# Rows of q and k moved straight from SBUF to the heads' rows, without a DRAM scratch, in a two-layer attention and pooling kernel

## The reference

```python
# layer 0, per batch: 16 heads of 16, s = side input, x = input
q = (s + b_self) @ Wq + bq            # 256 x 256, scaled by 1/4
k = (x + b_prev) @ Wk + bk;  v = x @ Wv + bv
k_self = (s + b_self) @ Wk + bk;  v_self = s @ Wv + bv
score_prev = q k^T (keys past the length masked);  score_self = sum(q * k_self) per head
w = softmax([score_prev, score_self]);  x1 = x + (w_prev @ v + w_self * v_self) @ Wo + bo
# layer 1: pooling with one of three masks per batch
t = tanh(x1 @ W1 + b1) . v;  p = softmax(masked t, per row);  out = x1 + (p @ x1) / count
```

## Time and profile before

| | us |
|---|---|
| median of three runs (range) | 279.0 (278.47 to 279.12) |
| the profiled execution: its own time | 281.62 |
| span from first to last instruction in its profile | 279.9 |
| TensorE busy / VectorE / ScalarE / GpSimd | 238.4 / 184.4 / 156.6 / 76.3 |
| mean granted TensorE clock | 0.950 of 2.4 GHz |
| busy in DMA queue q1, share of 16 engines' span | 44.6% |

### The profile page before, as it was taken

How to read it: one execution, slowest core, us unless ns; L and a number is a source line. 1 busy time by engine, 2 the same in 40 slices (tenths; PEclk the granted TensorE clock), 3 DMA queues, 4 the chain that set the end, 5 groups by cost and what they waited for, 6 DMA issues and landing times.

```text
span 279.9 us, 6089 instructions
## 1 busy us (share of the span) xinstructions
PE 238.4 (85%) x2100; PEld 187.4 (67%) x2100; DVE 184.4 (66%) x384; ACT 156.6 (56%) x297; POOL 76.3 (27%) x87
## 2 busy tenths in 40 slices
PE   2986898599979999999999989999999769886732
PEld 2984787367758777877788768777787455563622
DVE  2659655457469758875887588758985885335631
ACT  4351223376477557755785667557856546772430
POOL 8026011013025103610451035103511330316111
PEclk9999669599999999999999999999999997999977
DMA  5469636913865096609560946096409410011011
GB/s 152 103 235 233 138 112 182 210 31 115 242 142 188 5 248 134 228 16 252 119 227 20 256 108 225 18 246 118 150 33 261 95 72 2 8 34 37 0 40 37
DMA packets 28021, 35.50 MB, mean 127 GB/s; under 512 B 4440, under 2 KB 24416, under 8 KB 28000
## 3 DMA queue, kind: packets, MB, share of 16 engines
q1 hardware_dynamic: 27360, 33.12, 44.6%
q0 software_dynamic: 640, 2.10, 2.0%
HBM read 20.26 MB, written 14.69 MB: 125 GB/s over the span
## 4 chain that ended last, share of the span: by engine, by line
PE 59%; DVE 13%; DMA 9%; issue 8%; ACT 5%; SPq 3%; POOL 1%; ACTq 0%; DVEq 0%; POOLq 0%
PE ps_any L1080 20%; PE ps_any L1134 10%; PE ps_max L1108 9%; PE ps_any L1087 6%; DMA k_rows<-k_spill 5%; PE ps_exp L1121 4%; DVE s_max L887 4%; DMA k_spill<-k_lo 3%; PE ps_any L1184 3%; PE ps_any L1240 2%; DVE bv_cast L854 2%; SPq L418 1%; ACT pt L623 1%; PE ps_any L1200 1%; PE ps_any L1166 1%
## 5 line engine op out<-in xcount | busy, mean ns | idle before, releaser
L887 DVE TENSOR_REDUCE s_max<-ps_max 128x4 f32<-128x1024 f32 x64 | 78.1, 1220 | 25.1 <-PE ps_max L1108 25.1
L623 ACT ACTIVATE pt<-ps_exp 128x1024 f32<-128x1024 f32 x64 | 65.6, 1025 | 50.1 <-PE ps_exp L1121 49.5
L1108 PE MATMUL ps_max<-k_rows,q_rows 49*128 49x256 f32 x256 | 33.7, 343 | 13.0 <-DMA k_rows<-k_spill 7.2
L1108 PEld LDWEIGHTS ps_max<-k_rows,q_rows 49*128 49x128 f32 x256 | 20.2, 194 | 24.6 <-DVE s_max L887 10.4
L1134 PE MATMUL ps_any<-pt,v_aug 128*32 128x256 f32 x512 | 36.0, 401 | 0.0
L1121 PE MATMUL ps_exp<-q_rows,k_rows 51*128 51x256 f32 x256 | 27.0, 288 | 2.3 <-ACT pt L623 2.3
L578 POOL TENSOR_TENSOR attn<-num,rden 128x256 f32<-128x256 f32 x16 | 9.6, 621 | 54.0 <-DVE rden L1030 54.0
L1121 PEld LDWEIGHTS ps_exp<-q_rows,k_rows 51*128 51x128 f32 x256 | 20.3, 191 | 4.1 <-ACT pt L623 2.7
L569 POOL TENSOR_TENSOR prod_lo<-prod,prod_hi 128x512 fp32r<-128x512 f32 x8 | 10.3, 1282 | 42.2 <-ACT prod_hi L714 42.2
L1080 PE MATMUL ps_any<-st_hi,w_hi 128*128 128x256 f32 x64 | 20.9, 326 | 0.3 <-DVE st_lo L912 0.3
L1134 PEld LDWEIGHTS ps_any<-pt,v_aug 128*32 128x32 f32 x512 | 13.7, 112 | 10.5 <-issue 1.3
(11 more groups left out here) (145 smaller groups left out, 605.3 us busy)
## 6 DMA issues: line engine op xcount, KB each, us to landing
q_rows<-q_spill SPq DMA_DIRECT2D x32, 192.0 KB, 4.4
k_rows<-k_spill SPq DMA_DIRECT2D x32, 192.0 KB
q_spill<-q_hi SPq DMA_DIRECT2D x16, 256.0 KB, 2.5
k_spill<-k_hi SPq DMA_DIRECT2D x16, 256.0 KB, 2.5
s_sb<-in_fside_BxSxS SPq DMA_DIRECT2D x8, 256.0 KB, 3.7
x_sb<-in_x SPq DMA_DIRECT2D x8, 256.0 KB, 3.2
q_spill<-q_lo SPq DMA_DIRECT2D x8, 256.0 KB, 2.2
k_spill<-k_lo SPq DMA_DIRECT2D x8, 256.0 KB, 3.1
```

The source lines that it names most:

```text
L623: nc.scalar.activation(pt[:, 2 * j % 8:2 * j % 8 + 2], ps_exp[:], ACT.Exp).then_inc(p_ready, 1)
L887: nc.vector.tensor_reduce(s_max[:, j // MJ, :, :, j % MJ].rearrange("p t e -> p e t"), ps_max[:], AX.X, ALU.max).then_inc(max_found, 1)
L1108: last = pe.matmul(ps_max[:, e, t], q_rows[par][rows, j, P * t:P * t + P], k_rows[par][rows, j, :], start=True, stop=True)
```

## The change

The weight columns of q and k are ordered so that the half m of the projection is g, and a partition is (e, d, j within the half). A band of a head's rows then is 64 partitions of one part tile, and a DMA can move it from SBUF to SBUF: 64 partitions by 256 numbers become 16 partitions by 4 pairs by 256. The scratch, its spills and their semaphores are gone. Each batch now takes 12 such DMAs of 64 KB for q and 12 for k, next to the same two for the mask, where it took 6 spills and 8 placements before. q's g = 0 rows are sent ahead of the first half of the maxima, the others behind them in the order k 0, q 1, k 1. Tiles q_hi, q_lo, k_hi, k_lo are free again when both halves are placed, not when they are spilled. The biases of q and k come by four DMAs, not two. VectorE's set-up moves from the end of period -1 into steps 2, 4, 6 and 10 of period 0, and `bv_product` into its step 5.

```diff
-            def spill(i, k, parts, hi_done, lo_done, pattern, dram, placed, placed_per, spilled):
-                n_parts = held(count(i, k, 1, 1))
-                if (n := held(count(i, k, placed_per, 0))) is not None:
-                    for half in placed:
-                        sp.wait_ge(half, n)
...
-            def place(dram, rows, placed, g):
-                for e in range(2):
-                    sp.dma_start(rows[64 * e:64 * e + ROWS, MJ * g:MJ * g + MJ].bitcast(F32),
-                                 dram[e].rearrange("c (d j) t -> (c d) j t", d=DH)[:, MJ * g:MJ * g + MJ]
-                                 ).then_inc(placed[g], 16)
+            def place(part, rows, placed, g, threes):
+                for c in threes:
+                    for e in range(2):
+                        sp.dma_start(rows[64 * e + DH * c:64 * e + DH * c + DH, MJ * g:MJ * g + MJ].bitcast(F32),
+                                     part[P // 2 * e:P // 2 * e + P // 2, g, :].bitcast(F32)
+                                     ).then_inc(placed[g], 16)
+            def place_q(i, k, g):
+                par = k % 2
+                n_parts = held(count(i, k, 1, 1))
+                n_scored = held(count(i, k, NJ, MJ * (g + 1) - 2 * NJ))
+                if n_scored is not None:
+                    sp.wait_ge(scored, n_scored)
+                elif g == 0:
+                    sp.wait_ge(rows_one, par + 1)
+                sp.wait_ge(q_copied, n_parts)
+                place(q_hi, q_rows[par], q_placed, g, (0, 1))
+                sp.wait_ge(q_lo_done, n_parts)
+                place(q_lo, q_rows[par], q_placed, g, (2,))
+            def place_k(i, k, g):
...
+                sp.wait_ge(k_hi_done, n_parts)
+                place(k_hi, k_rows[par], k_placed, g, (0, 2))
+                if isinstance(i, int) and 2 * i + k == 0:
+                    sp.wait_ge(masks_stored, 16)
+                sp.dma_start(k_rows[par][R_MASK:R_MASK + 65:64, MJ * g:MJ * g + MJ].bitcast(F32), mask
+                             ).then_inc(k_placed[g], 16)
+                sp.wait_ge(k_lo_done, n_parts)
+                place(k_lo, k_rows[par], k_placed, g, (1,))
...
                 if live(*nxt):
-                    spill(*nxt, (q_hi, q_lo), q_copied, q_lo_done, (0, 0, 1), q_spill, q_placed, 32, q_spilled)
+                    place_q(*nxt, 0)
+                if live(*nxt) and not live(*b):
+                    place_q(*nxt, 1)
                 if live(*b):
                     place_max(*b, 0)
                 if live(*nxt):
-                    spill(*nxt, (k_hi, k_lo), k_hi_done, k_lo_done, (0, 1, 0), k_spill, k_placed, 48, k_spilled)
...
+                    place_k(*nxt, 0)
+                    if live(*b):
+                        place_q(*nxt, 1)
+                    place_k(*nxt, 1)
...
                 for n, vec in enumerate((bq, bk)):
-                    sp.dma_start(bqk_raw[:, n, :], vec.rearrange("(j e d) -> d j e", e=2, d=DH)
-                                 ).then_inc(bias_loaded, 16)
+                    for g in range(NM):
+                        half = vec.rearrange("(g n) -> g n", g=NM)[g]
+                        sp.dma_start(bqk_raw[:, n, g:g + 1], half.rearrange("(j f) -> f j", j=MJ).unsqueeze(2)
+                                     ).then_inc(bias_loaded, 16)
...
-                    if first and s == STEPS:
-                        cast_bv()
-                        weight_lo(3)
-                        setup_pooling()
-                        dve.wait_ge(bv_product_ready, 1)
-                        nc.vector.tensor_tensor(bias_out[:], bo_wide[:], ps_exp[:, 0, 0], ALU.add
-                                                ).then_inc(bias_out_done, 1)
+                    if isinstance(i, int) and 2 * i + k == 0:
+                        if s == 2:
+                            cast_bv()
+                        if s == 4:
+                            weight_lo(3)
+                        if s == 6:
+                            dve.wait_ge(bv_product_ready, 1)
+                            nc.vector.tensor_tensor(bias_out[:], bo_wide[:], ps_exp[:, 0, 0], ALU.add
+                                                    ).then_inc(bias_out_done, 1)
+                        if s == 10:
+                            setup_pooling()
...
+                    if isinstance(i, int) and (2 * i + k, s) == (0, 5):
+                        bv_product()
...
-                if first:
-                    bv_product()
```

More of the change, by code:

```diff
@@ new lines, in place_k @@
+            def place_k(i, k, g):
+                par = k % 2
+                mask = row(mask_dram, i, k).unsqueeze(0).unsqueeze(0).broadcast_to([2, MJ, S])
+                n_parts = held(count(i, k, 1, 1))
+                sp.wait_ge(k_hi_done, n_parts)
[6 more added lines that the diff above has]
+                place(k_lo, k_rows[par], k_placed, g, (1,))
@@ L530, in _, with split_lo @@
                                     pattern=[[-P, KB], [1, S]], channel_multiplier=-1).then_inc(pool_const, 1)
-            def split_lo(i, k, full_done, hi_done, full, hi, lo, lo_done, spilled):
+            def split_lo(i, k, full_done, hi_done, full, hi, lo, lo_done, placed):
                 pool.wait_ge(full_done, count(i, k, 1, 1))
                 pool.wait_ge(hi_done, count(i, k, 1, 1))
-                if (n := count(i, k, 48, 0)) is not None:
-                    pool.wait_ge(spilled, n)
+                if (n := count(i, k, 96, 0)) is not None:
+                    for half in placed:
+                        pool.wait_ge(half, n)
                 nc.gpsimd.tensor_tensor(lo[:], full[:], hi[:].bitcast(F32), ALU.subtract).then_inc(lo_done, 1)
@@ L555, in period @@
                     for c in at("q_lo", i, k, s):
[L556 removed]
+                        split_lo(*c, q_full_done, q_copied, q_full, q_hi, q_lo, q_lo_done, q_placed)
                     for c in at("x1_lo", i, k, s):
@@ L635, in weight_hi @@
                 for kb in range(KB):
-                    dst, src = w_hi[:, n, kb], w_raw[:, n, kb]
                     if n < 2:
[L638 to L641, removed]
+                        last = nc.scalar.activation(
+                            w_hi[:, n, kb].rearrange("p (g f j) -> p g f j", g=NM, j=MJ),
+                            w_raw[:, n, kb].rearrange("p (g j f) -> p g f j", g=NM, j=MJ),
+                            ACT.Copy, scale=QSCALE if n == 0 else 1.0)
+                    else:
+                        last = nc.scalar.activation(w_hi[:, n, kb], w_raw[:, n, kb], ACT.Copy)
+                    last.then_inc(w_hi_ready, 1)
             def period(i, k):
@@ L694, in period @@
                         act.wait_ge(k_ready, count(*c, 1, 1))
-                        if (n := count(*c, 48, 0)) is not None:
-                            act.wait_ge(k_spilled, n)
+                        if (n := count(*c, 112, 0)) is not None:
+                            for half in k_placed:
+                                act.wait_ge(half, n)
                         for m in range(2):
@@ L769, in q_copy @@
                 last.then_inc(q_full_done, 1)
-                if (n := count(i, k, 48, 0)) is not None:
-                    act.wait_ge(q_spilled, n)
+                if (n := count(i, k, 96, 0)) is not None:
+                    for half in q_placed:
+                        act.wait_ge(half, n)
                 for m in range(2):
@@ L793, in weight_lo @@
                     if n < 2:
-                        for e in range(2):
-                            hi, lo = (w[:, n, kb].rearrange("p (e d j) -> p e d j", e=2, d=DH)[:, e]
+                        for g in range(NM):
+                            hi, lo = (w[:, n, kb].rearrange("p (g f j) -> p g f j", g=NM, j=MJ)[:, g]
                                       for w in (w_hi, w_lo))
-                            src = w_raw[:, n, kb].rearrange("p (j e d) -> p e d j", e=2, d=DH)[:, e]
+                            src = w_raw[:, n, kb].rearrange("p (g j f) -> p g f j", g=NM, j=MJ)[:, g]
                             last = nc.vector.scalar_tensor_tensor(
@@ L990, in period @@
                         dve.wait_ge(k_hi_done, count(*c, 1, 1))
-                        if (n := count(*c, 48, 0)) is not None:
-                            dve.wait_ge(k_spilled, n)
+                        if (n := count(*c, 112, 0)) is not None:
+                            for half in k_placed:
+                                dve.wait_ge(half, n)
                         for m in range(2):
@@ L1160, in self_scores @@
             def self_scores(bank):
-                by_block = bank[:, 0, 0:2 * H].rearrange("p (g t e j) -> p t e g j", g=NM, t=KB, e=2)
+                by_block = bank[:, 0, 0:2 * H].rearrange("p (g t j) -> p t g j", g=NM, t=KB)
                 for t in range(KB):
-                    for e in range(2):
+                    for g in range(NM):
                         for part in (prod_hi, prod_lo):
```

(2 more changed lines are left out.)

18 lines of the change are left out of this document (5 added, 13 removed).

## The result

| | before | after |
|---|---|---|
| median of the runs taken side by side (range), four each | 278.7 us (276.6 to 279.1) | 297.0 us (293.9 to 298.0) |
| ratio, with its 95% interval | | 1.065 (1.056 to 1.075): slower |
| the profiled execution: its time / its span | 281.62 / 279.9 | 298.02 / 296.3 |
| mean granted TensorE clock in it | 0.950 | 0.918 |

Forecast was 273.0 us, with a chance of 0.11 for slower; the time lies 19 us above the range. Of the rivals only D, "283.6 or more", pointed this far, by a mechanism that is not the one found.

A forecast was written before the change was run, and what follows sets the result against it. It took TensorE, busy for 85% of the span, as the bound, with waits for k rows. Terms -1.1 + 1.7 + 0.9 - 3.15 - 1.8 - 2.1 - 0.4 = -5.95 us took 279.0 to 273.0 us; range 269.3 to 278.0.

The forecast's parts named there:

- D: Rival for the row DMAs: write rate falls in full proportion, 0.92 us a DMA; 283.6 us or more, chance 0.10.
- what stands last in SP's queue: SP's queue: free 12.5 us after the copy, the second maxima next, landing in time by half a microsecond.
- From the third period on ... what the change does to DMAs there is hidden: TensorE has no idle time worth the name there; periods 3 and later stay at 27.8 us.
- Issue of 0.50 us: SP's issuing of each new 64 KB row DMA: 0.50 us taken, with 0.65 kept as a rival.
- rival E: SP's queue: issuing costs 0.65 us a DMA, the second maxima come late; 279.5 us, no change, chance 0.10.
- Landing of 2.6 us: Each row DMA lands 2.6 us from the start of its issue, within 2.2 to 4.2.
- B: Rival for the row DMAs: narrow writes pace the queue at 0.61 us a DMA; 274.5 us, chance 0.15.
- Waits of periods 1 and 2: TensorE's waits for k rows at these periods' starts: both go, 3.15 and 2.12 us.
- The start: Period 0's start: last k_lo issued at 25.1, landed at 27.7 against 28.18; max0 gains only 0.5 us.
- The clock: TensorE in period 1: without the wait at 49.2 the clock should not fall at 51, worth 1.8 us.
- Set-up in period 0: Moved work costs 1.7 us for `bv_product` and 0.9 us for the small set-up ahead of max5's reduction.
- the gain of 1.1 us: Start of period 0: without set-up ahead, the first Q product starts at 30.1 and not 31.20.

The follow-up runs named there:

- e1: The changed kernel with the reload of x issued right behind the next batch's loads, ahead of the row DMAs: 286.2 us, ratio 1.023 to the kernel before.
- e4: The kernel before with nine more 8 KB DMAs, which nothing reads, ahead of the reload in each period: 293.6 us, ratio 1.046.
- e5: e4 with the reload of x moved ahead of the row DMAs, so the nine no longer precede it: 282.5 us, ratio 1.005.
- e6: e1 with k's g = 0 rows sent ahead of q's g = 1 rows in period -1 too: 281.0 us, ratio 1.004 to the kernel before.
- e3: The changed kernel with VectorE's set-up and bias product put back at the end of period -1: 298.1 us, ratio 1.068 to the kernel before.
- e8: The kernel before with groups of four DMAs of several forms behind its last store: SBUF-to-SBUF forms took 0.59 to 0.62 us to issue.
- e2: The kernel before with only VectorE's set-up and the bias product moved into period 0: 280.7 us, ratio 1.008.
- e11: The kernel before with further DMA groups behind its last store: the 256 KB spill stayed below 0.5 us to issue, 128 into 128 partitions in SBUF took 0.60.

## Why the prediction was wrong, step by step

**The failed step: what stands last in SP's queue.** The prediction worked out when SP is free, "free at 1.4 + 3.6 + 6.6 + 0.9 = 12.5 us after the copy", with "a load or two, 0.9" in it, and then asked only for "the next thing in the queue", the second maxima. The reload of x is one of those loads, and it stands behind all row DMAs. Where the time was read as free, there was a customer: GpSimd's `x_bo` had 25.0 us of waits for it before. Shown by e1 (10.9 us back by moving it), by the chain, and by e4 and e5 without any new path. The other 7.4 us of the 18.3 lie outside this step: e6 gives some 5 back by the order at the start.

**"From the third period on ... what the change does to DMAs there is hidden".** Wrong for the same reason. TensorE had no idle time there, but it has no slack either: periods 3 to 6 became 11.3 us longer. That x1 comes late, and that GpSimd's heap of work then meets `hidden`, is seen in the rows above. Periods 2 and 3 suggest that the first alone costs little; no run took the two apart.

**Issue of 0.50 us: the mis-sized term.** A row DMA takes 0.59 us at the median, and 0.63 from one to the next (2.50 for four). That is rival E's price (0.65), and the maxima's 0.63 were the nearer row, not a spill's 0.49. E had the right resource and sized it at 279.5, with the maxima as its victim. In the kernel after exp's waits for them sum to 0.8 us, in e3 to 5.7; the greater victim, the reload, it did not name.

**Landing of 2.6 us.** Right: 2.6 at the median, 2.4 to 3.6, by SP's DMAs of line 395. Rivals B and D, that narrow writes go slowly, are out. B's 0.61 us a DMA is near the pace measured, but not for B's reason: the share of the DMA engines was 0.28 from 24.5 to 30.4 us (windows below), where SP sent such DMAs one behind the other, and in e8 64 partitions into 64 took 0.60 us to issue, as 64 into 16 did.

**Waits of periods 1 and 2: a second mis-sized term.** The waits for k rows are gone, as predicted, but the sum booked them whole, -3.15 and -2.1. TensorE also waits there for VectorE's reduction of max7, which the rows' lateness had covered: in the kernel before the one at 76.66 us ended 1.5 us after TensorE ran dry. With the rows in time 0.99 and 1.68 us of wait remain, and the five other runs with direct rows have 0.99 to 1.18 and 1.68 to 1.69 us in the same places. So the two terms were worth about 2.2 and 0.4 us. P0 is 1.1 us shorter. P1 is 1.7 us longer, as TensorE's busy time in it grew by 2.2 us at a clock of 0.83 instead of 0.92.

**The start.** Predicted 27.7 for max0, got 30.42. The last k_lo of g = 0 was issued at 27.70 and not 25.1, 2.6 us later: 17 row DMAs at 0.63 and not 0.50, with the mask's, make 2.3 of it. e6 shows that the order cost as much as the price: with k's rows ahead of q's second half, max0's reduction came 3.1 us earlier than in e1.

**The clock.** "If the wait at 49.2 is gone, the clock should not fall at 51" failed. Windows of the kernel after (stretch, length; busy PE, PEld, DVE, ACT, POOL; clock; DMA share, GB/s):

```profile
24.50:30.40 5.90, 0.01 (x1) 0.01 (x1) 0.00 (x0) 0.60 (x1) 0.82 (x1) 0.90 0.28 96
30.40:36.80 6.40, 6.38 (x32) 5.37 (x32) 4.93 (x9) 1.50 (x3) 0.00 (x0) 0.56 0.39 131
36.80:47.00 10.20, 9.05 (x67) 7.76 (x66) 8.60 (x27) 3.41 (x10) 2.53 (x2) 0.97 0.17 60
47.00:63.30 16.30, 14.44 (x81) 10.75 (x80) 8.29 (x15) 6.56 (x10) 0.00 (x0) 0.50 0.29 96
```

The clock was at half, 1.2 GHz, for about 6 us behind the long wait at the start, and for the 16.3 us from 47.0, where before it was 10.1 and 4.8 us. Ahead of the fall there is no wait for rows; the longest gap of TensorE was 0.93 us, at max5. The kernel before and e3 have the same gap (0.94 us at 43.69 and 43.82) and stayed at full clock behind it, so the gap doesn't tell them apart. In e3, which differs only by the set-up, the clock stays at 1.00 from 44 to 56 us and P0 is 3.5 us shorter, but P1 2.8 us longer. That the moved set-up brings the fall is not shown: the clock fell to half once between 42 and 59 us in all eleven versions without a probe, with the set-up moved at 42 to 49 us, without at 42 to 59, and stayed there for 3 to 17 us. What sets the moment and the length stays open.

**Set-up in period 0.** The cast's 4.64 us became 0.48, as the Trainium skill's rule (SBUF — State Buffer, Who interferes with whom) has it: VectorE's two-port instruction and GpSimd's exclude each other. The trace agrees here and at `hidden`, 2.76 against 0.48 us. But the gain of 1.1 us that the prediction booked beside it was swallowed, since the k rows came later than the set-up ended. `setup_pooling` ran from 44.14 to 47.04, ahead of the reduction of max5, as predicted. By the prediction's own terms the whole part was -1.1 + 1.7 + 0.9 = +1.5 us; e2 measured +1.3 us by the medians, +2.1 by the ratio. The sum fits, but its terms aren't confirmed: e2's profiled execution shows a P0 0.9 us shorter than before, not longer, and a span of 278.1 us. The agreement can be luck.

**Issue against transfer.** The Trainium skill (DMA: Bandwidth & Descriptors, Issuing engines are not separate DMA queues) says of a DMA's initiation on the sequencer that it is "usually small relative to the DMA itself". Here it was 0.63 of 2.6 us each, which isn't small beside it, and landings overlap while issues don't: 24 row DMAs and two for the mask had SP issuing for some 16 us of every period of about 30.

**What stays open.** From the last max0 to the end the six kernels with direct rows took 63.0 to 64.8 us in their profiled executions, the five with the scratch (without the two probes) 59.5 to 63.9. The granted clock there was 0.85 to 0.86 in the six and 0.86 to 0.96 in the five; in the kernel after TensorE's busy time there is 2.9 us longer than before, more than the 2.1 us of the table. No run took the reason apart. Open as well is why the clock was lower in periods 4 and 6 of the kernel after; it goes with the late reload, as e4 has 0.95 and 0.94 there too and e1 has 1.00.

## What to carry to other kernels

When an edit turns few large DMAs into many small ones on one queue, count the issues, and price each by a row of the same two memories and the same number of partitions: by memories alone the rows here run from 0.42 to 0.60 us from DRAM, and from 0.47 to 0.60 us to DRAM. When a wait is to go, look for what else ends inside it: only the part behind that is won. Then walk the queue to its last entry, and ask of each who waits for it, above all of loads that other engines use. A DMA whose inputs are ready early belongs ahead of a block of row DMAs. An engine without idle time isn't a proof that nothing late can reach it.

## What the runs showed of the hardware that was not expected

- Issuing on SP took 0.59 to 0.62 us for every SBUF-to-SBUF form from 8 to 128 KB, whether 8 or 128 partitions, folded or not. From DRAM it took 0.42 us into 16 partitions, 0.43 us into 128 and 0.60 us into 64; to DRAM 0.60 us from 64 partitions and 0.47 us from 128, for the 256 KB spill (e8, e11).
- Narrow rows were no burden to the DMA engines: 64 KB into 16 partitions landed in 2.6 us, and q1's share fell by half, with 38% fewer bytes.
- A 7.9 us wait of GpSimd, on an engine that is busy for a quarter of the span, made an instruction of another engine 1.5 us longer than before the change (2.76 against 1.24 us; 0.48 us where GpSimd is idle), by moving more of its work on top of it.
